# Adaptive-layernorm block with attention and experts: gate weights stationary, negated maxima copied first, attention's 32 groups written out

## The reference

```python
h = _layernorm(x, axis=-1) * (1 + ca) + sa
x = x + ga * attn(h)              # 16 heads of 32, causal softmax, q/k/v/o projections with biases
h = _layernorm(x, axis=-1) * (1 + cb) + sb
x = x + gb * ffn(h)

# ffn(h)
logits = flat @ gate_w.T          # 8192 tokens x 32 experts
scores = jax.nn.sigmoid(logits)
topk_idx, topk_w = route_tokens(scores, bias_corr)   # 4 of 8 groups, then 4 experts
...                               # each expert keeps its first 256 tokens
h = relu2(jnp.einsum('ecd,ehd->ech', xe, up_w))
ye = jnp.einsum('ech,edh->ecd', h, down_w)
shared = relu2(hidden_states @ shared_up_w.T) @ shared_down_w.T
return routed + shared
```

## Time and profile before

| | us |
|---|---|
| median of 3 runs | 3359.95 |
| lowest and highest | 3357.3, 3363.82 |
| the profiled execution's own time | 3366.32 |
| span of its trace | 3364.6 |

### The profile page before, as it was taken

One profiled execution on the slowest core, in us unless ns is written; L12 is line 12 of the kernel. 1 busy time (PEld: TensorE's weight loads), 2 busy tenths in 40 slices (PEclk: granted clock), 3 DMA queues, 4 the chain that ended last, 5 costly groups with the idle time before them and its releaser, 6 DMA issues. The chain is left out here.

```text
span 3364.6 us, 58432 instructions
## 1 busy us (share of the span) xinstructions
PE 3092.1 (92%) x17008; PEld 2268.2 (67%) x17008; DVE 2144.3 (64%) x5319; ACT 1380.3 (41%) x2739; POOL 1911.0 (57%) x1121
## 2 busy tenths in 40 slices
PE   3999999799999999999999939999999999985997
PEld 1888888555555655655655427888888888865775
DVE  3545555277656766766677344777777877864665
ACT  1222222146555655655666613323323323324665
POOL 2322323147767766767777834466566576554665
PEclk7999999889989998989999969999999999997998
DMA  8455555654445545444555033233233233217997
GB/s 169 161 201 192 193 178 174 176 121 103 103 104 116 124 108 115 103 104 103 113 126 120 19 117 122 67 110 100 66 109 100 75 100 100 66 38 197 231 234 138
DMA packets 297724, 420.07 MB, mean 125 GB/s; under 512 B 64775, under 2 KB 148743, under 8 KB 297494
## 3 DMA queue, kind: packets, MB, share of 16 engines
q1 hardware_dynamic: 274974, 383.70, 41.3%
q0 software_dynamic: 22528, 33.72, 5.3%
HBM read 262.85 MB, written 153.01 MB: 124 GB/s over the span
## 5 line engine op out<-in xcount | busy, mean ns | idle before, releaser
L684 POOL TENSOR_TENSOR att_pt<-att_pt 128x2048 f32<-128x2048 f32 (+3 forms) x288 | 895.5, 3109 | 382.1 <-PE att_ps_o L834 367.6
L727 ACT ACTIVATE att_pt<-att_ps_p 128x512 f32<-128x512 f32 (+3 forms) x1536 | 685.7, 499 | 549.3 <-PE att_ps_p L879 345.9
L760 DVE CUSTOM_DVE_ANT_0 att_ps_s<-att_ps_s,att_causal 128x512 f32<-128x512 f32 (+3 forms) x1024 | 492.4, 505 | 186.3 <-PE att_ps_s L824 182.9
L876 PE MATMUL att_ps_p<-att_qs,att_ks 98*128 98x512 f32 (+3 forms) x1536 | 573.3, 397 | 31.5 <-issue 23.2
L824 PE MATMUL att_ps_s<-att_ks,att_qs 96*128 96x512 f32 (+3 forms) x1536 | 506.6, 388 | 23.0 <-DMA att_ks<-qk_parts 22.3
L876 PEld LDWEIGHTS att_ps_p<-att_qs,att_ks 98*128 98x128 f32 x1536 | 298.7, 196 | 337.9 <-ACT att_pt L727 201.7
L766 DVE TENSOR_REDUCE att_lower<-att_ps_s 128x1 f32<-128x512 f32 x512 | 351.8, 687 | 206.6 <-PE att_ps_s L824 205.1
L824 PEld LDWEIGHTS att_ps_s<-att_ks,att_qs 96*128 96x128 f32 x1536 | 290.0, 202 | 77.9 <-issue 22.7
L834 PE MATMUL att_ps_o<-att_pt,att_vs 128*32 128x512 f32 (+3 forms) x3072 | 339.0, 515 | 0.0
L1146 POOL DMA_INDIRECT slot_info<-ffn_info,ffn_slot x256 | 270.0, 1055 | 114.8 <-issue 77.0
L311 POOL TENSOR_TENSOR qkv_x<-qkv_x,qkv_mod 128x512 f32<-128x512 f32 x64 | 91.1, 1424 | 363.1 <-DVE qkv_x L378 363.1
(11 more groups left out here) (254 smaller groups left out, 6352.4 us busy)
## 6 DMA issues: line engine op xcount, KB each, us to landing
att_qs<-qk_parts SPq DMA_DIRECT2D x96, 512.0 KB, 6.9
att_ks<-qk_parts SPq DMA_DIRECT2D x96, 512.0 KB, 12.7
qk_parts<-qkv_out_hi SPq DMA_DIRECT2D x128, 256.0 KB, 2.6
qk_parts<-qkv_out_lo SPq DMA_DIRECT2D x128, 256.0 KB, 2.9
qkv_x<-x SPq DMA_DIRECT2D x16, 1024.0 KB, 5.7
v_rows<-qkv_out_v SPq DMA_DIRECT2D x64, 256.0 KB, 2.3
att_vs<-v_rows SPq DMA_DIRECT2D x32, 512.0 KB, 16.0
o_parts<-att_o SPq DMA_DIRECT2D x64, 256.0 KB, 7.2
```

Of the source, the lines that this page charges most:

```text
L684: pool.tensor_tensor(into, into, tile(c)[:, :, col:UNIT], ALU.add).then_inc(add_done, 1)
L727: act.activation(tile(c)[:, h, col:UNIT], ps_p[n % NP][:, col:UNIT], ACT.Exp, scale=float(HD) ** -0.5).then_inc(exp_done, 1)
L760: dve.tensor_tensor_reduce(bank, bank, causal[:, UNIT - (c1 - c0):UNIT], scale=1.0, scalar=MASKED, op0=ALU.add, op1=ALU.max, accum_out=row ...
L876: last = pe.matmul(ps_p[n % NP][:, col:UNIT], ks[prev.slot][:, h, kt * P:(kt + 1) * P], qs[prev.slot][:, h, q0:(qh + 1) * UNIT], start=Tru ...
```

## The change

In attention:

- `steps` has no loop: all steps are written out, on all engines.
- PE's `turn` is issued at the start of chunk 10, ahead of its first probability matmul, instead of behind the second.
- SP issues the copy of `m_hi` as soon as `m_hi` is there, then waits for `m_lo` and copies it; `pack(prev, 0)` now follows them.
- DVE's inversions move from chunks 2 and 9 to 3 and 11.

In the FFN stage:

- The gate weights are stationary (64 or 32 columns) and 512 tokens move: 8 matmuls into `ps_t[0]`, logits with experts on partitions.
- ACT copies them to a new tile `gateT` (64 x 512), and behind the first up piece PE transposes that back with 4 transposes into `ps_g`. From there ACT and DVE go on as before, with semaphore counts to match.

```diff
@@ stage_attention
-        LATER = (2, 9)
+        LATER = (3, 11)
...
         def steps(step):
-            BODY = 2 * SLOT
-            LOOPS = (GROUPS - 3) // BODY
-
             def run(eng):
                 first = Group(0, 0, 0)
                 step(first, None)
-                step(first.ahead(1), first)
-                with eng.Fori(0, LOOPS) as i:
-                    for j in range(BODY):
-                        prev = Group(i * BODY, 0, i * (BODY // SLOT)).ahead(j + 1)
-                        step(prev.ahead(1), prev)
-                for g in range(LOOPS * BODY + 1, GROUPS):
+                for g in range(GROUPS):
                     prev = first.ahead(g)
                     step(prev.ahead(1) if g + 1 < GROUPS else None, prev)
             return run
...
                 if prev:
                     store(prev, 0)
-                    pack(prev, 0)
                 if cur:
-                    sp.wait_ge(mlo_done, CREDIT + cur.g + 1)
-                    for row, part in ((STACK, m_hi), (STACK + 1, m_lo)):
+                    for row, part, done in ((STACK, m_hi, mhi_done), (STACK + 1, m_lo, mlo_done)):
+                        sp.wait_ge(done, CREDIT + cur.g + 1)
                         sp.dma_start(raw(qs[cur.slot][row:row + 1, :, :]).rearrange("o h (q t) -> o (h q) t", q=KT),
                                      raw(part[:, :])).then_inc(m_in[cur.slot], 16)
+                if prev:
+                    pack(prev, 0)
...
                     if c == 0:
                         pe.wait_ge(m_in[prev.slot], CREDIT + 32 * (prev.use + 1))
                         pe.wait_ge(v_in[prev.slot], CREDIT + 16 * (prev.use + 1))
+                    if cur and c == TURN:
+                        turn(cur, prev)
                     for h in range(GH):
...
-                        if cur and c == TURN and h == 1:
-                            turn(cur, prev)
@@ stage_project_route_shared
+        gateT_sb = s.sb("gateT", [2 * NE, UNIT], FP32)
...
-                act.wait_ge(gate_done, CREDIT + u + 1)
+                act.wait_ge(gate_done, CREDIT + 2 * u + 1)
+                act.activation(gateT_sb[:, :], ps_t[0][0:2 * NE, :], ACT.Copy).then_inc(cross_done, 1)
+                act.wait_ge(gate_done, CREDIT + 2 * u + 2)
                 act.activation(logits[:, :, :], gate_parts[:, :, NE:2 * NE], ACT.Copy).then_inc(cross_done, 1)
...
-                dve.wait_ge(cross_done, CREDIT + u + 1)
+                dve.wait_ge(cross_done, CREDIT + 2 * u + 2)
...
-                pe.wait_ge(logit_done, CREDIT + u)
-                for t in range(UT):
-                    cols = slice(t * P, (t + 1) * P)
-                    both, high = ps_g[:, 2 * t * NE:2 * (t + 1) * NE], ps_g[:, 2 * t * NE:(2 * t + 1) * NE]
-                    for k in range(DK - 1):
-                        pe.matmul(both, hT_hi[:, k, cols], gt[:, k, :], start=k == 0, stop=False)
-                    for k in range(DK):
-                        pe.matmul(high, hT_lo[:, k, cols], gt_hi[:, k, :], start=False, stop=False)
-                    last = pe.matmul(both, hT_hi[:, DK - 1, cols], gt[:, DK - 1, :], start=False, stop=True)
-                last.then_inc(gate_done, 1)
+                both, high = ps_t[0][0:2 * NE, :], ps_t[0][0:NE, :]
+                for k in range(DK - 1):
+                    pe.matmul(both, gt[:, k, :], hT_hi[:, k, :], start=k == 0, stop=False)
+                for k in range(DK):
+                    pe.matmul(high, gt_hi[:, k, :], hT_lo[:, k, :], start=False, stop=False)
+                pe.matmul(both, gt[:, DK - 1, :], hT_hi[:, DK - 1, :], start=False, stop=True).then_inc(gate_done, 1)
...
+                    if n == 0:
+
+                        pe.wait_ge(cross_done, CREDIT + 2 * u + 1)
+                        pe.wait_ge(logit_done, CREDIT + u)
+                        pe.sem_inc(mark, 1)
+                        for t in range(UT):
+                            last = pe.transpose(ps_g[:, 2 * t * NE:2 * (t + 1) * NE], gateT_sb[:, t * P:(t + 1) * P], ident[0:2 * NE, 0:2 * NE])
+                        last.then_inc(gate_done, 1)
```

## The result

| | before | after |
|---|---|---|
| median, us | 3361.89 (4 runs, 3357.3 to 3366.24) | 3258.11 (4 runs, 3255.63 to 3261.94) |
| span of the profiled execution, us | 3364.6 | 3260.2 |
| mean granted clock | 0.935 | 0.958 |

The ratio is 0.9693, 95% interval 0.9655 to 0.973: 3.1% faster, 104 us. Forecast were 3240, from 3222 to 3280.

A forecast was written before the change was run, and what follows sets the result against it. PE's stream was taken as the bound almost everywhere, partly at half clock. Attention's 66 us and the FFN stage's 54 make 120 off the profiled 3366.3, so 3246; the median, 6.4 lower, was predicted as 3240, range 3222 to 3280.

The forecast's parts named there:

- Part 1, no loop: Attention: 30 written-out steps take 36.99 us each like the straight code of before; 54.0 us less.
- Part 2, maxima first: Attention's seams: earlier turn and copies bring a step to 36.6 us, near nothing for clean steps, late copies 0.5 earlier.
- The sum for attention: Attention, turn 0 to turn 31: written-out steps and early maxima together give 1137 us, 66 less.
- Part 3, the gate: FFN gate block: 8 matmuls in 1.8 us and transposes in 0.44 replace 3.65; 1.4 us less a unit.
- My bound of 0.2 below: FFN gate: lower end of 0.2 us for the four new transposes, with 0.44 as the upper end.
- The cover: FFN units: the first up piece, 2.7 us, hides PE's wait for ACT's copy; failure would cost 10 us.
- Part 4, the clock: Behind the FFN gate block: no clock fall, units of 58.9 us; 33 of the stage's 54 us.
- Nothing elsewhere: Start to turn 0, turn 31 to gate block 1, experts to the end: 0 us difference each.
- Falls in the FFN stage behind the block: Rival: the clock still falls once in each FFN unit because of the transposes; 3273 us, chance 0.08.
- Stalls at fetches: Rival in attention: written-out code stalls at instruction fetches as the loop body does; 3267 to 3300 us, chance 0.07.
- Early copies do nothing: Rival in attention: the maxima's early copies win nothing, the step stays at 36.99 us; 3252 us, chance 0.05.
- Slower: Rival in attention: PE's new stand plus the seam's wait make the clock fall each step; 3414 us, chance 0.04.

The follow-up runs named there:

- E2: Kernel before with attention's steps written out and nothing else changed; 3387.66 us, ratio 0.9841.
- E4: Kernel before with only attention's maxima part (early turn, copies first, inversions in chunks 3 and 11), loop and gate as before; 3413.85 us, ratio 0.9899.
- E12: Kernel after with the turn back behind the second probability matmul of chunk 10, copies still ahead of the packing; 3249.81 us, one run.
- E5: Kernel after itself, unchanged, run again on another chip; 3361.48 us, ratio 0.9666 to the kernel before there.
- E8: Kernel after with each of the four gate transposes issued four times, 16 in all; 3399.88 us, one run.
- E11: Kernel after with each of the four gate transposes issued eight times, 32 in all; 3280.91 us, one run.
- E10: Kernel before with its 32 narrow gate matmuls cut into two halves, ahead of and behind the first up piece; 3347.41 us, one run.
- E7: Kernel after with four spare 16 KB DMAs on SP ahead of the maxima's copies in each step; 3618.72 us, one run.
- E6: Kernel after with the turn behind the first probability matmul of chunk 10 instead of ahead of it; 3342.7 us, ratio 0.9624.

## Right and wrong, point by point

The forecast, 120 us less, was too large by 15.6 against the spans' 104.4; the time came out 18 us above it and inside the range.

- **Part 1, no loop: cause right, size too small.** 39.24 to 36.99 a step was expected, 54 us. E2 has 67.1, with three late steps. The step that failed is taking the six straight steps as what straight code costs. They were four that met an instruction fetch behind the turn and two that didn't, and in E2's code the fetches lie elsewhere. The size of E2's 67.1 has some 10 us of scatter in it, by the loop steps of the other traces. The difference of 1.08 us of idle time between the two kinds stood in the earlier trace rows, and its cause could have been looked up in the DMA view.
- **Part 2, maxima first: the sign of one half wrong.** It was costed as near nothing in a clean step, a stand of 0.25 against a gain of 0.36. The stand was right (0.30). The gain wasn't there: a clean straight step of before has 36.34 busy in 36.43, so there was no idle time to win; the 0.36 was that of loop steps. In E4's loop, where that time was there, the forecast came true: 36.55 to 36.61 a clean step, against 36.48 to 36.61 before. In straight code the clean step went from 36.47 (E2) to 36.71. The other half, copies ahead of the packing with the later inversions, was right and is worth 36.47 to 36.3, and part of the late steps besides (E12).
- **The sum for attention** (66) came near 60.5 since the two errors have opposite signs: 67.1 for the loop and 6.6 given back, 4.8 of it in the 30 steps with the early turn. The first step added 1.4 of its own (40.58 against 39.15, clock 0.77 against 0.81); E5, E8 and E11, whose attention is the same, have 38.3 to 38.7 there, so that I take it for chance. That the sum came near is in part luck.
- **Part 3, the gate.** The block was forecast at 1.8 and takes 1.85 for its eight matmuls; the transposes, forecast at 0.44, take 0.58. My bound of 0.2 below was wrong: by E11 an added one costs 0.062 us, but the first four cost 0.58, so some 0.33 is what the change of kind costs once. The gain is 1.13 a unit instead of 1.4, 4 us over 15 units. The cover held in units 1 to 15, with no wait ahead of the transposes; in unit 0 it failed by 1.48 us, which is in the 75.3 us that unit 0 takes.
- **Part 4, the clock.** Right, mechanism and size, though the mechanism was stated too firmly (in E2 and E4 17 of 30 old blocks have no fall): a unit without the fall was read as 60.3, and E10 shows 60.39; 33 us for 15 units were forecast, 31 for 14, and 29.5 measured for 14. Unit 0 gained nothing, as said (gate block 0 to 1 takes 74.6 and 75.3).
- **Nothing elsewhere** was wrong by 5.8 us: the untouched stages are 1.7, 2.3 and 1.8 us longer in this one profile. E12's pieces (turn 0 at 690.8, turn 31 to block 1 195.3, the experts 306.6) are like it, E11's (687.3, 195.6, 303.4) partly not. No cause was found.
- **Rivals.** Falls in the FFN stage behind the block: none in units 1 to 15 (unit 15 has one 28.5 us later). Stalls at fetches: they exist, as late copies, and the three chances for them in this kernel cost 0.3 us together. Early copies do nothing: wrong for the copies, but the early turn took back more than they won, 36.47 to 36.71 a clean step. Slower: shown by E7 to be a real mechanism at 1.7 us of idle time; the kernel has none, so it stayed out.

## A version that beats both

The kernel after with the turn in its old place (E12) took 3249.81 us in one run, and its profile is 12 us shorter than that of the kernel after (3248.1 against 3260.2), on another chip. E6, nearly the same edit, was 3342.7 against 3361.48 beside it. What is shown is the 10.6 to 13 us in attention, of which 10.8 (E5 to E6) and 11.6 (E12) lie in the 30 steps behind the first; the size over the whole kernel isn't settled to better than that.

## What to carry to other kernels

A short idle time of the matmul engine costs little by itself and much by the clock that it may bring down; so cost a seam by its idle time first. In attention here stands from 1.0 us on carried a risk; in the FFN stage most of 2 us did not, so the bound of one stage isn't that of another. Before a stretch of straight code is taken as the model of written-out code, look in the DMA view at which of its pieces met an instruction fetch. When a test finds no fall of the clock behind a suspect stretch, look first at whether plain idle time of that length brings one in the same stage. When an instruction is moved forward in an in-order stream to help a later transfer, price the stand that it causes against the time by which the transfer really starts earlier, here 0.30 against 0.22 us.

## What the hardware showed unexpectedly

- **Other DMAs are late beside a fetch of instructions.** One fetch of 16 KB takes 0.9 to 1.4 us in most cases, and a 16 KB copy under way beside it landed 1.0 us later (3.1 against 2.1). In the loop of before it met the same step in each of the four iterations. Back edges cost 3.15 to 3.95 us of idle PE in the four traces with the loop, also where the copies are early (3.65 in E4), and nothing once the loop is gone. This agrees with the Trainium skill (Runtime: NRT & Kernel Launch, Instruction fetch mechanics), by which a taken branch out of the fetched pages forces a fetch before execution goes on.
- **Pieces that are taken late.** On the two other chips ACT takes PE's finished pieces late in the FFN stage. In E5 PE runs without a gap, and from 2166.18 ACT takes its pieces every 2.72 us, until one comes 5.9 us behind the last. Below are the busy times of PE there, ACT's timeline, and a row of ACT's waits over 800 us of the stage; the kernel after on the first chip has no such row.

```profile
2165.00:2176.00 11.00, 11.00 (x51) 1.00 0.03 3
```

```profile
2166.18 0.60 ACT L1189 ACTIVATE ffn_relu<-ffn_ps_m 128x512 f32<-128x512 f32 x1 [1.08 <-PE ffn_ps_m L1411]
2168.90 0.60 ACT L1189 ACTIVATE ffn_relu<-ffn_ps_m 128x512 f32<-128x512 f32 x1 [1.08 <-issue]
2174.78 0.60 ACT L1189 ACTIVATE ffn_relu<-ffn_ps_m 128x512 f32<-128x512 f32 x1 [4.25 <-PE ffn_ps_m L1411]
```

```profile
ACT ffn_relu L1189 <- remote: 80.8, 20, 9.8
```

In the worst cases PE stands behind it, as I read it for want of a free bank, and the clock falls. Units with the new gate are 60 to 70 us there instead of 59.27. Unit 1 has none of it. Every kernel had these stalls on those chips and none on the others, so that they are no part of the change; their cause stays open.
